# A gated attention and mixture-of-experts layer: tiles of 128 places with held split weights become pairs of 256 places with weights split each time, and the first stage is rewritten

## The reference

```
x = x + tanh(g_xattn) * (attention(layernorm(x), ctx, ctx) @ W.T + b)   # 4 x 1024 rows of 256, 77 context rows each
xf = layernorm(x).reshape(4096, 256)
top_w, top_i = top_k(softmax(xf @ router_w.T), 2)        # 8 experts, 2 for each row, weights normed to sum 1
g = xf @ w_gate[e].T ; u = xf @ w_up[e].T                # 256 -> 512
y = (silu(g) * u) @ w_down[e].T                          # 512 -> 256
x = x + tanh(g_ffn) * sum over the 2 chosen e of weight * y
```

## Time and profile before

| | before |
|---|---|
| median of 3 runs | 479.53 us (474.03 to 480.17) |
| profiled execution: time | 478.07 us |
| profiled execution: span | 476.2 us |
| mean granted clock of TensorE | 0.909 |
| TensorE busy | 422.5 us (89%) |
| TensorE weight loads busy | 356.2 us (75%) |
| VectorE busy | 239.4 us (50%) |
| ScalarE busy | 192.2 us (40%) |
| GpSimd busy | 242.1 us (51%) |

### The profile page before, as it was taken

How to read it: one execution, slowest core, us unless ns; L and a number is a source line. 1 busy time by engine, 2 the same in 40 slices (tenths; PEclk the granted TensorE clock), 3 DMA queues, 4 the chain that set the end, 5 groups by cost and what they waited for, 6 DMA issues and landing times.

```text
span 476.2 us, 9017 instructions
## 1 busy us (share of the span) xinstructions
PE 422.5 (89%) x2491; PEld 356.2 (75%) x2492; DVE 239.4 (50%) x748; ACT 192.2 (40%) x480; POOL 242.1 (51%) x310
## 2 busy tenths in 40 slices
PE   7988886630669999999999999999999999999994
PEld 3847665420448888888888888888888898888884
DVE  3115899989935555555555543333333333333331
ACT  2353655302024555454545543343433333343331
POOL 8421676753053555265645555556554645555552
PEclk9595889555589999999999999999999999999999
DMA  6714566688521333833543334243333332423342
GB/s 196 234 46 133 192 214 219 211 284 274 210 70 22 49 67 49 305 55 57 105 124 60 56 56 66 47 67 51 62 55 57 48 63 45 67 45 56 56 66 27
DMA packets 31943, 49.59 MB, mean 104 GB/s; under 512 B 3516, under 2 KB 25489, under 8 KB 31921
## 3 DMA queue, kind: packets, MB, share of 16 engines
q0 software_dynamic: 13152, 18.65, 23.6%
q1 hardware_dynamic: 17511, 29.84, 18.6%
q10 hardware_dynamic: 1258, 0.84, 0.6%
HBM read 31.76 MB, written 17.57 MB: 104 GB/s over the span
## 4 chain that ended last, share of the span: by engine, by line
PE 77%; DVE 11%; DMA 3%; ACT 3%; issue 2%; POOL 2%; POOLq 0%; SPq 0%; ACTq 0%; DVEq 0%
PE GT L1088 19%; PE Y L1115 19%; PE UP L1088 19%; PE HT L1105 6%; PE S L997 4%; PE XT L1079 3%; PE O L1030 3%; DVE at_low L766 2%; DVE at_tile L877 2%; DMA out_rows<-y,idx 2%; ACT ex L559 1%; DVE xg L795 1%; DMA kr<-in_router 1%; DVE st L799 1%; PE O L1016 1%
## 5 line engine op out<-in xcount | busy, mean ns | idle before, releaser
L499 POOL DMA_INDIRECT out_rows<-y,idx x67 | 107.7, 1608 | 141.5 <-ACT y L625 90.2
L1115 PE MATMUL Y<-w_high,hT 128*128 x536 | 107.1, 283 | 0.0
L1088 PE MATMUL GT<-w_high,xtT 128*128 x272 | 102.7, 418 | 0.4 <-issue 0.4
L1088 PE MATMUL UP<-w_high,xtT 128*128 x272 | 102.0, 416 | 0.0
L930 DVE TENSOR_TENSOR hT<-HT,hT 128x512 fp32r<-128x512 f32 x67 | 46.4, 692 | 107.2 <-ACT hT L619 107.2
L491 POOL DMA_INDIRECT xt<-xn_rows,idx x71 | 70.9, 999 | 38.3 <-issue 20.7
L1115 PEld LDWEIGHTS Y<-w_high,hT 128*128 128x128 f32 x536 | 87.7, 190 | 3.0 <-issue 0.3
L625 ACT ACTIVATE y<-Y,xt 128x256 f32<-128x256 f32 x67 | 31.8, 474 | 139.8 <-PE Y L1115 114.3
L1115 PE MATMUL Y<-w_low,hT 128*128 x268 | 67.2, 283 | 0.0
L920 DVE TENSOR_TENSOR xtT<-XT,xtT 128x256 fp32r<-128x256 f32 x69 | 29.3, 425 | 59.6 <-ACT xtT L611 59.5
L1088 PEld LDWEIGHTS GT<-w_high,xtT 128*128 128x128 f32 x272 | 51.4, 189 | 10.3 <-issue 0.9
(11 more groups left out here) (158 smaller groups left out, 531.5 us busy)
## 6 DMA issues: line engine op xcount, KB each, us to landing
raw<-in_weights SPq DMA_DIRECT2D x16, 768.0 KB, 6.6
xn_rows<-pay SPq DMA_DIRECT2D x8, 528.0 KB, 3.2
xTg<-in_xT SPq DMA_DIRECT2D x8, 512.0 KB, 5.9
xg<-in_x SPq DMA_DIRECT2D x8, 512.0 KB, 5.1
out_rows<-xg SPq DMA_DIRECT2D x8, 512.0 KB, 3.3
xt<-xn_rows,idx POOLq DMA_INDIRECT x71, 2.8
out_rows<-y,idx POOLq DMA_INDIRECT x67, 3.8
kr<-in_ctx_rows SPq DMA_DIRECT2D x1, 308.0 KB
```

The costliest lines, as they stand in the source:

```text
L499: gp.indirect_dma_start(out=out, out_offset=bass.IndirectOffsetOnAxis(ap=idx[:, j:j + 1], axis=0), in_=y[:, j % 2, :], in_offset=None, com ...
L1088: last = mm(bank[:], xtT[:, s % 2, px, c * P:(c + 1) * P], parts[pw][c][:, bass.ds(e * HW + k * HID, HID)], start=(c == 0 and n == 0), sto ...
L1115: last = mm(Y[:, s % 2, 0:D], hT[:, px, c * P:(c + 1) * P], parts[pw][c // (HC // DC)][:, bass.ds(e * HW + DOWN + c % (HC // DC) * D, D)], ...
```

## The change

The expert stage works on pairs of 256 places (`PT`). The weights are stationary and the turned pair moves, 256 columns; so `GT` and `UP` come out with the hidden dimension on partitions, and no hidden transposes are left. The split weights are no longer kept: for each pair ScalarE casts and VectorE subtracts 3 x 1024 elements a partition (`cut_gate_up` for each half q of the hidden, `cut_down`), into `gu` (one buffer for each half) and `dn` (two buffers). `raw` holds all experts; the last four are loaded in 16 pieces, one after each pair's gather. There are four `y` buffers, and adds are still one after another, two a pair; the skewed case is gone. The hidden goes through SBUF: silu, times `UP`, cast, subtraction.

In the first stage the keys of batch 0 go ahead of the others, masks are made on VectorE, the bias comes by an addition in place of a product, values of batches 2 and 3 are computed inside the groups, the scaling by the reciprocal sum moves from GpSimd to the row add on VectorE, the mean of the attended rows comes from a ninth router column, their variance from a sum of squares on ScalarE (`sum_squares2`), and rows of `at_low` stand between dependent small instructions of VectorE. `at_tile` is made by four instructions. TensorE's filler products (`keep_busy`) are 20, 4, 3 and 4 in the head, up to 5 of 512 columns in a group, and 22 after the list. The tables of experts are computed after `idx`.

The diff, cut to what the prediction speaks of:

```diff
-TILES = (TOPK * N - NE) // P + NE
-TW = TILES + 1
+PT = 2 * P
+PAIRS = (TOPK * N - NE) // PT + NE
+LEAST = TOPK * N // PT
+TILES = 2 * PAIRS
...
-XR = 8
-AHEAD = 6
+XR = 4
+AHEAD = 3
...
+            for e in range(4, NE):
+                for part in range(PARTS):
+                    j = AHEAD + PARTS * (e - 4) + part
+                    sp.wait_ge(tile_loaded[j % XR], 32 * (j // XR + 1))
+                    load_weights(e, range(part, part + 1))
...
+            def gather(j, t):
...
+            def add(j, t):
+                pool.wait_ge(y_added, 16 * (2 * j + t) + Y_ADDED0)
+                pool.wait_ge(y_ready, 2 * j + t + 1 + Y_READY0)
+                gp.indirect_dma_start(
+                    out=out, out_offset=bass.IndirectOffsetOnAxis(ap=idx[:, 2 * j + t:2 * j + t + 1], axis=0),
+                    in_=y[:, j % 2, t, :], in_offset=None, compute_op=ALU.add).then_inc(y_added, 16)
...
+            for j in range(LEAST):
+                for t in range(2):
+                    gather(j + AHEAD, t)
+                for t in range(2):
+                    add(j, t)
...
+            def sum_squares2(k):
+                act.wait_ge(negmean2_ready, k + 1)
+                for t in range(G):
+                    act.wait_ge(rows_added, k * G + t + 1)
+                    last = nc.scalar.activation(squares2[:, t], rows(k, t), ACT.Square, bias=negmean2[:, k % 2, t:t + 1],
+                                                accum_out=ssq[:, k % 2, G + t:G + t + 1])
+                last.then_inc(ssq2_ready, 1)
...
+                sum_squares2(k)
+                if k == 0:
+                    sum_squares(n, every)
+                inverse_sqrt(n)
+                if n + 1 < GROUPS:
+                    sum_squares(n + 1, front)
+                if n < GROUPS:
+                    exponentials(n)
                 exp_gap(k)
...
+            def cut_gate_up(j, e, q):
+                act.wait_ge(up_ready, 2 * j + q - 1)
+                nc.scalar.copy(gu[:, 0, q], gate_up_of(e, q)).then_inc(gu_high[q], 1)
+            def cut_down(j, e, b):
+                act.wait_ge(down_ready, 2 * j - 2 + DOWN0)
+                nc.scalar.copy(dn[:, 0, b], down_of(e)).then_inc(dn_high, 1)
...
+            def hid_highs(j, q):
+                act.wait_ge(hid_ready, 2 * j + q + 1 + HID0)
+                nc.scalar.copy(hT[:, 0, 2 * q:2 * q + 2], hid[:, q]).then_inc(hid_high, 1)
             def weigh(j, s, e):
+                for t in range(2):
+                    act.wait_ge(y_added, 32 * j + 16 * t - 48 + Y_ADDED0)
+                    act.wait_ge(down_ready, 2 * j + t + 1 + DOWN0)
+                    nc.scalar.mul(y[:, s % 2, t], Y[:, t, 0:D], xt[:, 2 * s + t, bass.ds(e + CW, 1)]).then_inc(y_ready, 1)
...
+            def turn(j, s, i, known=None, behind=2):
+                e, e1 = known or (weights_of(j), weights_of(j + 1) if behind > 0 else None)
+                e2 = None
+                if behind > 0:
+                    act.wait_ge(raw_loaded, 16 * PARTS * (e1 + 1))
+                    cut_gate_up(j + 1, e1, 0)
+                hid_highs(j, 0)
+                silu(j, 1)
+                if behind > 1:
+                    tile_highs(j + 2, s % 2)
+                hid_highs(j, 1)
+                if behind > 0:
+                    silu(j + 1, 0)
+                    cut_gate_up(j + 1, e1, 1)
+                    cut_down(j + 1, e1, (s + 1) % 2)
+                if behind > 1 and s < XR - 1:
+                    e2 = weights_of(j + 2)
                 weigh(j, s, e)
...
+                def add_rows(t):
+                    return stt(out=rows(k, t), in0=O[:, t // 2, t % 2 * D:(t % 2 + 1) * D], scalar=rg[:, q, t:t + 1],
+                               in1=rows(k, t), op0=ALU.mult, op1=ALU.add)
+                scaled = mark(tt(out=lg0[:], in0=M[:, 0:G * RW].rearrange("p (t e) -> p t e", t=G),
+                                 in1=rg[:, q].unsqueeze(2).to_broadcast([P, G, RW]), op=ALU.mult))
+                add_rows(0).then_inc(rows_added, 1)
+                after(scaled)
+                summed = mark(tt(out=lg1[:], in0=lg0[:], in1=sr[:, q], op=ALU.add))
+                add_rows(1).then_inc(rows_added, 1)
+                after(summed)
+                ts(negmean2[:, q], lg1[:, :, NE], -1.0 / D, None, ALU.mult).then_inc(negmean2_ready, 1)
+                add_rows(2).then_inc(rows_added, 1)
+                add_rows(3).then_inc(rows_added, 1)
+                behind = -1 if k == GROUPS - 1 else k - 2
+                at_lows(behind, range(0, 2))
+                if k == 0:
+                    negated_means(n)
+                    reciprocal_sums(1)
+                else:
                     share(k - 1)
+                if n + 1 < GROUPS:
+                    negated_means(n + 1)
                 if more:
                     reduced = maxima(n)
+                    router_part(n)
+                if k > 0:
+                    own = own_ranks(k - 1)
+                    at_lows(behind, range(2, 3))
+                    ranked = unit_ranks(k - 1, own)
+                    at_lows(behind, range(3, 4))
+                    masked = low_bits(k - 1, ranked)
+                    at_lows(behind, range(4, 5))
+                    low_places(k - 1, masked)
+                dve.wait_ge(ssq2_ready, k + 1)
                 if more:
+                    dve.wait_ge(ssq_ready, n + 1)
+                    ts(ve[:, q], ssq[:, q], float(D) * EPS, None, ALU.add).then_inc(var_ready, 1)
...
+                at_lows(behind, range(5, 8))
...
                 refine(n)
                 if more:
...
+            for c in range(0, UNITS, CHUNK):
+                tt(out=at_tile[:, c:c + CHUNK], in0=iota_t[:].unsqueeze(1).to_broadcast([P, CHUNK, TILES]),
+                   in1=col[:, c:c + CHUNK].unsqueeze(2).to_broadcast([P, CHUNK, TILES]),
+                   op=ALU.is_equal).then_inc(tile_hot, 1)
...
+            def cut_gate_up(j, e, q):
+                dve.wait_ge(gu_high[q], j + 1)
+                low_of(gu[:, 1, q], gate_up_of(e, q), gu[:, 0, q]).then_inc(gu_low[q], 1)
+            def cut_down(j, e, b):
+                dve.wait_ge(dn_high, j + 1)
+                low_of(dn[:, 1, b], down_of(e), dn[:, 0, b]).then_inc(dn_low, 1)
+            def gate_up(j, q):
+                dve.wait_ge(silu_ready, 2 * j + q + 1 + SILU0)
+                dve.wait_ge(up_ready, 2 * j + q + 1)
+                wide = hid[:, q].rearrange("p h t -> p (h t)")
+                tt(out=wide, in0=wide, in1=UP[:, q], op=ALU.mult).then_inc(hid_ready, 1)
+            def hid_lows(j, q):
+                dve.wait_ge(hid_high, 2 * j + q + 1)
+                low_of(hT[:, 1, 2 * q:2 * q + 2], hid[:, q], hT[:, 0, 2 * q:2 * q + 2]).then_inc(hid_low, 1)
...
+            def turn(j, s, i, e=None, behind=2):
+                gate_up(j, 0)
+                if behind > 0:
+                    e1 = weights_of(j + 1)
+                    cut_gate_up(j + 1, e1, 0)
+                hid_lows(j, 0)
+                gate_up(j, 1)
+                if behind > 1:
+                    tile_lows(j + 2, s % 2)
+                hid_lows(j, 1)
+                if behind > 0:
+                    cut_gate_up(j + 1, e1, 1)
+                    cut_down(j + 1, e1, (s + 1) % 2)
...
             transpose_exp(0)
-            pe.wait_ge(vw_copied, BATCH)
+            values(1)
             attention(0)
+            scores(2)
             transpose_exp(1)
-            scores(2)
+            scores(3)
             for k in range(GROUPS):
                 if k > 0:
                     ranks(k - 1)
-                if k + 3 < GROUPS:
-                    scores(k + 3)
+                if k + 1 < GROUPS:
+                    pe.wait_ge(rows_added, (k + 1) * G)
+                    attention(k + 1)
+                if k < 2:
+                    values(k + 2)
+                elif k + 2 < GROUPS:
+                    pe.wait_ge(vw_copied, BATCH)
+                    keep_busy(3)
                 if k + 2 < GROUPS:
                     transpose_exp(k + 2)
+                if k + 4 < GROUPS:
+                    scores(k + 4)
+                if 2 <= k < GROUPS - 2:
+                    keep_busy(2)
...
+            def first_layer(bank, b, q, w):
+                for h in range(2):
+                    for c in range(DC):
+                        for n, (px, pw) in enumerate(HI_LO):
+                            last = mm(bank[:, h * PT:(h + 1) * PT], gu[:, pw, q, c, w, h * P:(h + 1) * P], xtT[:, b, px, c],
+                                      start=(c == 0 and n == 0), stop=(c == DC - 1 and n == 2))
+                return last
+            def gate(j, b, q):
+                pe.wait_ge(gu_low[q], j + 1)
+                pe.wait_ge(silu_ready, 2 * j + q - 1 + SILU0)
+                first_layer(GT[:, q], b, q, 0).then_inc(gate_ready, 1)
+            def up(j, b, q):
+                pe.wait_ge(hid_ready, 2 * j + q - 1 + HID0)
```

(60 more changed lines are left out.)

837 lines of the change are left out of this document (376 added, 461 removed).

## The result

The changed kernel takes 461.9 us (median of 4 runs, 457.7 to 467.2) where the kernel before takes 479.9 in the same comparison: ratio 0.963, 95% interval 0.952 to 0.974. The prediction was 454 us, range 433 to 476, faster. Its profiled execution took 462.32 us (span 460.6), that of before 478.07 (span 476.2).

A forecast was written before the change was run, and what follows sets the result against it. VectorE bounded the groups; in the experts TensorE was back to back, the adds close behind. First add at 120.2 us (148.7 - 14.5 - 9 - 5), 327 us of adds, 5.15 after, 1.9 more: 454 us, range 433 to 476.

The forecast's parts named there:

- (a): Experts: the indirect adds bound a pair at 9.6 us, 454 us in all; chance 0.5.
- (b): Experts: TensorE bounds the pair, as adds land sooner without a gather between and meet no subtraction; 435 us, chance 0.17.
- (c): Groups: TensorE's clock at half over four to six groups, +18 to +28 us, 472 to 481 us; chance 0.13.
- Head: Up to the first rows of group 0: these come at 25 us instead of 39.50, -14.5 us.
- Groups: From group 0 to group 7: seven intervals shrink from 8.9 to 7.3 us, taken as -9 us in all.
- ScalarE becomes the bound: Groups: ScalarE's work rises from 5.03 to 7.1 us, 7.3 with waits, while VectorE falls from 8.35 to 7.1.
- End: From group 7 to the first add: fewer at_low rows there and at_tile at 5.9 against 9.57 us, together -5 us.
- The first add stays as far behind the list as before: Start of the experts: two gathers, a longer cast and subtraction (+0.5 us) against no hidden transposes (-0.6).
- TensorE: Experts: TensorE needs 9.05 us a pair against 9.74 for two tiles before.
- The adds: nothing makes one cheaper: Experts: two serial adds a pair at 4.6 us each, 9.2 us, exceed TensorE's 9.05 and become the bound.
- Subtractions beside adds: Experts: adds starting inside VectorE subtractions with two SBUF inputs take longer, 0.4 us a pair, bounds 0 and 2.4.
- Weights: Experts: weight pieces of 0.39 MB, one a pair, meet adds' transfers and cost 5 us in all, bounds 0 and 10.

The follow-up runs named there:

- experiment 4: Changed kernel with the value products of batches 2 and 3 back in front of the first attention, on TensorE and VectorE: 461.5 us, one run.
- Experiments 1 and 2: Each on the changed kernel: 12 filler products for TensorE in groups 0 and 1 (453.5 us); VectorE combines values of batches 2 and 3 later (453.3 us).
- three_repairs: Changed kernel with 12 fillers in groups 0 and 1, values combined later, first silu earlier, and fillers between groups and experts: 449.7 us, ratio 0.944.
- experiment 8: Changed kernel with GpSimd's two waits ahead of an add in the earlier order, y first and landing second: 492.3 us, one run.
- experiment 9: Changed kernel with ScalarE's first silu ahead of the second tile cast and TensorE's second transposes between gate and up: 453.8 us, one run.
- experiment 5: Changed kernel with every second indirect add left out, so its output lacks half of the contributions: 444.2 us, one run.
- experiment 6: Changed kernel with the weights of experts 4 to 7 loaded right behind expert 3, without waiting for tiles: 454.2 us, ratio 0.954.

## Why the prediction was right, and where its steps failed

**Direction and range** held. The likeliest case did not occur: instead of (a) both (b), in the experts, and (c), in the groups, came true in the main, and they largely cancel. That the total fell near the forecast, and in the range, is luck in that sense.

**Head:** right in this profile, 24.26 for 25 us, and 2 to 3 us too cautious in the others, 22.1 to 22.9. My reading of the head of before was off: the earlier trace rows has half clock in only the second of its first four slices, and of the value products only the first ran at half clock. By experiment 4, 2 us or more of the 15 are only moved into the groups.

**Groups: the step that failed by most.** "ScalarE becomes the bound", 7.3 us, was wrong in two ways. Where the clock is full, VectorE bounds them at 7.9 to 8.0 (7.51 of 8 us busy, predicted 7.1; ScalarE's 6.71 lie below its 7.1). And groups 1 to 3 ran at half clock and took 10.4 to 15.4 us. There a score group on the chain takes nearly twice what it took before the clock fell:

```profile
27.03 1.95 PE S L1057 x16
...
37.08 3.66 PE S L1057 x16
```

Rival (c) had +18 to +28 us from the half clock alone, with a chance of only 0.13 because of "denser work". The groups came 20.5 over the forecast, but fillers gave back 10.7 of that, so the clock was about half of it. The work was not denser for TensorE: it was busy 8.53 of 10 us just before the clock fell, and 9.60 with the fillers. I had also costed the value products in the groups at nothing but TensorE's room. Their combination on VectorE made a wait in the turn, 5.68 us in group 1. Experiments 1 and 2 each give back some 8 us of the median, and in the groups hardly more together (62.1 us in three_repairs, 63.3 with the fillers alone), since they cure the same stretch. What is left over the forecast's 53.5 is 0.6 to 0.7 us in each group that VectorE bounds, and the first group, 10.8 to 11.6 us at full clock in every run; why that one is long was not followed up.

**End:** -3.9 for -5. at_tile took 5.48 (predicted 5.9) and the list came 8.1 us nearer to group 7, but the first add 4.2 us further behind the list. "The first add stays as far behind the list as before" failed. Half clock on gate and up (2.54 and 2.08 us on the chain) is no new cost in itself, for the kernel before had it there too (2.19 and 2.16). New are a silu that starts 3.0 us after gate has ended, where it followed at once, two gathers ahead of the first transposes instead of one, and 0.55 us for the wait for y, now the last of two (experiment 8). Experiment 9 takes back some 1 to 2 us.

**TensorE:** right, 9.12 for 9.05 us a pair (experiment 5).

**The adds: the second step that failed.** "The adds: nothing makes one cheaper" took 4.6 us from the earlier trace rows. But the diff also exchanges the two waits ahead of an add, and that is worth 0.5 us at each landing that is waited for (experiment 8). A pair is 4.1 to 4.2 us for a landing and 5.0 for GpSimd's own issues, an add and two gathers: 9.1 to 9.2 in all. So the adds just keep up with TensorE, as rival (b) had it, and only every second one waits for a landing, where I expected all to. The gathers, which I gave no term of their own, fill the other half. My reading in the earlier trace rows, "noticed some 0.8 us after it", was exact. What I did not ask was what made the 0.8. Without the exchange the stage took 348.8 us in one run, above the 327 forecast and the 322.3 of before, and the kernel 492.3. So the two lines decide whether the change gains at all.

**Subtractions beside adds:** the term was 0.4 us a pair. Its size was about right and its place wrong. The adds' median is 1.62 us against 1.59; 21 of the 68 start inside a subtraction of two SBUF inputs and take 0.17 us longer on the mean. Most of it falls on gathers: 35 of 74 start inside one, with 0.55 us of it left on the mean, and take 0.46 us longer. Here one takes 1.54 us, where the next takes 0.98:

```profile
354.38 1.23 DVE L975 TENSOR_TENSOR gu<-raw,gu 128x1024 fp32r<-128x1024 f32 x1 [1.20 <-ACT gu L632]
```

That is nearly 0.5 us a pair, and it is paid, since the next pair's first add stands right behind the two gathers. By the rule of the Trainium skill, "SBUF — State Buffer", "Who interferes with whom", a GpSimd instruction that reads SBUF contends with a VectorE instruction that has two SBUF inputs, for ports with an exclusive lock; the gathers agree (in the row above 0.66 us of the subtraction were left, and the gather took 0.56 longer). The 1.2 us a pair that I worked out from the rule was too much, since fewer than two of the four issues met a subtraction.

**Weights:** 5 us predicted, 5.0 between two profiles (experiment 6), with a spread from run to run that is larger than that.

## What to carry to other kernels

When GpSimd waits for two events ahead of an indirect DMA, put the wait for the late one first: the order of two lines was worth 34 us of the experts' stage here, in one run of each (24 us against the longest such stage with the good order). Follow each new wait in a turn between engines through to TensorE, and read TensorE's clock in any stretch that gets shorter: fillers in two groups gave back 10.7 us. A sum that comes out right may hide two errors, so check each of its terms.

## What the runs showed of the hardware that was not expected

- GpSimd starts an indirect add 0.27 us after the landing it waits for when that wait is the first of two, and 0.79 us when it is the last; with a wait for y it is 0.29 and 0.84 (experiment 8). Why is not shown: the trace has only "issue" there.
- TensorE's clock fell to half (1.2 GHz) in stretches where it had been busy 8.53 of 10 us just before (24 to 34 us, then 0.52), and stayed full (2.4 GHz) until 52 us where 12 fillers were put into each of two groups (busy 9.60 of 10 us, then 15.48 of 16). It can also move: with the same fillers and the value products in the head it fell 20 us later, at about 55 us.
- A gather that starts inside a VectorE subtraction of two SBUF inputs takes longer by nearly what is left of it: 0.46 us for 0.55 left, the mean of 35 in the changed kernel.
- The paced weight pieces of 0.39 MB delay some adds and not others: 309.9 us from first add to last without them, 313.6 to 324.3 with them in five kernels that have the same experts' code. Which pairs they hit was not settled.
